# Folded constant's base part by POOL and VectorE, second half's mask ahead of the first fold, both first x2 roundings on ScalarE

## What is computed

```
x = x + L0: x @ ((sum_g y[b,g] * weight[g]) * mask).T + bias              # L0_cond_bias
x = x + L1: x @ W_base.T + b_base + 2 * (((x @ As.T) * y) @ Bs)           # LoRA of rank 16, 8 experts
x = x + L2: top-2 mixture of 8 gelu experts (width 512) + a shared expert
x = x + L3: one silu expert of width 256, chosen by argmax, with biases
```

```
c_b = (I + W_base) bias_l0  +  Bs.T ( cond_scaled[b] * (As bias_l0) )  +  b_base
```

## Time and profile before

| | |
|---|---|
| median of 3 runs | 139.98 us |
| runs | 138.63 to 140.18 us |
| the profiled execution: time | 138.68 us |
| the profiled execution: span | 136.9 us |
| TensorE matmuls busy | 132.6 us |
| VectorE busy | 102.2 us (75%) |
| ScalarE busy | 99.3 us (73%) |
| POOL busy | 75.3 us (55%) |

### The profile page before, as it was taken

The page is one execution under the profiler, slowest core; times in us unless marked ns, Lnnn a source line. Parts: engine busy times, 40 slices in busy tenths (PEclk is TensorE's granted clock), DMA queues, the critical chain, the costliest instruction groups (busy, mean ns, idle before and its releaser), DMA issues.

```text
span 136.9 us, 3163 instructions
## 1 busy us (share of the span) xinstructions
PE 132.6 (97%) x866; PEld 121.0 (88%) x866; DVE 102.2 (75%) x201; ACT 99.3 (73%) x205; POOL 75.3 (55%) x89
## 2 busy tenths in 40 slices
PE   6999999999999999999999999999999999999991
PEld 5978887878888899999999999999999999999990
DVE  0699898797766677578886787867868677887792
ACT  3774797969964669777797777756757669889870
POOL 0238369776991046477486774863542635325770
PEclk9999999999999999999999999999999999999999
DMA  4999999997001976564774656746577476565134
GB/s 139 343 403 408 409 400 397 403 400 304 4 0 74 385 304 266 229 255 187 306 290 180 268 217 279 287 186 268 208 286 296 171 306 242 210 249 226 41 115 153
DMA packets 11345, 34.54 MB, mean 252 GB/s; under 512 B 1088, under 2 KB 2368, under 8 KB 11328
## 3 DMA queue, kind: packets, MB, share of 16 engines
q1 hardware_dynamic: 11184, 34.21, 63.8%
q10 hardware_dynamic: 144, 0.13, 0.3%
HBM read 12.32 MB, written 1.05 MB: 98 GB/s over the span
## 4 chain that ended last, share of the span: by engine, by line
PE 97%; DVE 0%; issue 0%
PE up L293 34%; PE gate L293 32%; PE acc L293 31%; DVE x_res L997 0%; DVE slabs L827 0%; DVE shift_pick L828 0%
## 5 line engine op out<-in xcount | busy, mean ns | idle before, releaser
L766 POOL TENSOR_TENSOR dn_lo<-slabs,dn_hi 128x256 fp32r<-128x256 f32 x40 | 29.7, 742 | 41.0 <-ACT dn_hi L649 41.0
L625 ACT ACTIVATE h_act<-gate 128x512 f32<-128x512 f32 x48 | 28.8, 599 | 26.6 <-PE gate L293 25.2
L917 DVE TENSOR_TENSOR h_pair<-up,h_pair 128x512 fp32r<-128x512 f32 x55 | 37.5, 682 | 0.0
L927 DVE SCALAR_TENSOR_TENSOR up<-h_act,w_route,up 128x512 f32<-128x512 f32 x32 | 24.2, 755 | 16.9 <-PE up L293 16.9
L293 PE MATMUL gate<-x_hi,w_gu 128*128 128x256 f32 x160 | 35.3, 281 | 0.0
L293 PE MATMUL up<-x_hi,w_gu 128*128 128x256 f32 x158 | 34.9, 282 | 0.0
L631 ACT ACTIVATE h_pair<-up 128x512 fp32r<-128x512 f32 x55 | 32.8, 596 | 0.0
L293 PEld LDWEIGHTS gate<-x_hi,w_gu 128*128 128x128 f32 x160 | 27.5, 188 | 0.2
L293 PE MATMUL acc<-h_pair,dn_hi 128*128 128x512 f32 (+1 forms) x76 | 27.6, 378 | 0.0
L293 PEld LDWEIGHTS up<-x_hi,w_gu 128*128 128x128 f32 x158 | 27.1, 188 | 0.0
L293 PE MATMUL gate<-x_lo,w_gu 128*128 128x256 f32 x80 | 22.5, 282 | 0.0
(11 more groups left out here) (127 smaller groups left out, 204.1 us busy)
## 6 DMA issues: line engine op xcount, KB each, us to landing
w_gu<-slabs SPq DMA_DIRECT2D x40, 512.0 KB, 3.0
slabs<-slabs_moe SPq DMA_DIRECT2D x8, 768.0 KB, 13.1
slabs<-slabs_l SPq DMA_DIRECT2D x4, 768.0 KB, 8.4
outT<-x_res SPq DMA_DIRECT2D x7, 128.0 KB, 2.0
sh_raw<-slabs_shared SPq DMA_DIRECT2D x2, 384.0 KB, 5.2
x_res<-x_rest SPq DMA_DIRECT2D x1, 768.0 KB, 7.0
slabs<-second_in SPq DMA_DIRECT2D x1, 320.0 KB, 3.1
slabs<-third_in SPq DMA_DIRECT2D x1, 256.0 KB, 3.8
```

The source lines that it names most:

```text
L625: nc.scalar.activation(h_act[:, u % 2, :], gate_ps[u % 2][:], ACT.Gelu_apprx_tanh).then_inc(act_done, 1)
L766: nc.gpsimd.tensor_tensor(dn_lo[:, q % W_SLOTS, :], slab_cols(at, DOWN_AT, 256), dn_hi[:, q % W_SLOTS, :].bitcast(F32), ALU.subtract).then ...
L917: V.tensor_tensor(h_lo[:, u % H_SLOTS, :], h_of(u), h_hi[:, u % H_SLOTS, :].bitcast(F32), ALU.subtract).then_inc(h_lo_done, 1)
L927: ins = V.scalar_tensor_tensor(h_of(u), h_act[:, k, :], weight, h_of(u), ALU.mult, ALU.mult)
```

## The change

The constant's base part leaves TensorE. The host passes `L0_cond_bias` copied to all partitions as a row, and `W_base` untransposed. POOL multiplies two rows of 128, the A rows and W_base, by the bias row; VectorE sums each over its 128 inputs. The first sum is `As bias_l0` (one number per rank row), and `a_bias_y` is `cond_scaled` times it. The second is `W_base bias_l0`, and a new [128, 1] tensor `c_base` is it plus `bias_l0` plus `b_base`. TensorE keeps one of three 8-column products.

A transposed is no longer loaded. The A rows move from the third input to the fourth; the third shrinks to 192 KB, the fourth grows to 320 KB. The first `lora` on TensorE now waits for the fourth input.

`mask_w0(1, 2, 6)` moves ahead of the two first folds on VectorE. The second `x_hi` rounding moves from VectorE to ScalarE, behind the first and ahead of `round_shared(1)`.

```diff
         second_sb = early(5, P)
-        third_sb = early(4, P)
-        fourth_sb = early(3, P)
+        third_sb = early(3, P)
+        fourth_sb = early(5, P)
+        bias_terms = early(2, P)
...
-        lora_bT, mask, lora_a = second_sb[:, 4, :], third_sb[:, 2, :], third_sb[:, 3, :]
-        w_baseT, ident, lora_aT = (fourth_sb[:, k, :] for k in range(3))
+        lora_bT, mask = second_sb[:, 4, :], third_sb[:, 2, :]
+        w_baseT, ident, bias_row, lora_a = (fourth_sb[:, k, :] for k in range(4))
...
+            pe.wait_ge(d_fourth, DMA)
+
             def lora(out, first_b, n):
...
             lora(gate_ps[0][:, 0:S], 0, 2)
-            pe.wait_ge(d_fourth, DMA)
-            mm(acc_ps[:, 512:512 + B], lora_aT, bias_l0.to_broadcast([P, B]), True, True).then_inc(a_bias_sum, 1)
             pe.wait_ge(bw_ready, 2)
...
-            pe.wait_ge(base_ready, 1)
             pe.wait_ge(a_bias_ready, 1)
-            mm(acc_ps[:, 0:B], base_i[:], bias_l0.to_broadcast([P, B]), True, False)
-            mm(acc_ps[:, 0:B], lora_bT, a_bias_y[:], False, True).then_inc(c_sum, 1)
+            mm(acc_ps[:, 0:B], lora_bT, a_bias_y[:], True, True).then_inc(c_sum, 1)
...
             nc.scalar.activation(x_hi[:, 0:S], x2_ps(0), ACT.Identity, bias=c_b[:, 0:1]).then_inc(x2_hi_half, 1)
+            act.wait_ge(x2_first_sum, 2)
+            nc.scalar.activation(x_hi[:, S:2 * S], x2_ps(1), ACT.Identity, bias=c_b[:, 1:2]).then_inc(x2_hi, 1)
             round_shared(1)
...
             nc.gpsimd.tensor_tensor(base_i[:], ident, w_baseT, ALU.add).then_inc(base_ready, 1)
+            nc.gpsimd.tensor_tensor(bias_terms[:, :, :], fourth_sb[:, 3:5, :], rows(bias_row, 2),
+                                    ALU.mult).then_inc(bias_terms_ready, 1)
             pool.wait_ge(hit_ready, 1)
...
-            dve.wait_ge(a_bias_sum, 1)
-            V.tensor_tensor(a_bias_y[:], acc_ps[:, 512:512 + B], cond_scaled[:], ALU.mult).then_inc(a_bias_ready, 1)
             mask_w0(0, 2, 6)
+            dve.wait_ge(bias_terms_ready, 1)
+            V.tensor_reduce(bias_in[:], bias_terms[:, :, :], AX_X, ALU.add).then_inc(bias_in_ready, 1)
+            dve.wait_ge(bias_in_ready, 1)
+            V.tensor_scalar(a_bias_y[:], cond_scaled[:], bias_in[:, 0:1], None, ALU.mult).then_inc(a_bias_ready, 1)
+            mask_w0(1, 2, 6)
             dve.wait_ge(r1_first, 2)
             for b in range(2):
                 dve.wait_ge(m_first_sum, b + 1)
                 V.tensor_tensor(m_b[:, b, :], m_first_banks[b], r1_b[:, b, :], ALU.add).then_inc(m_first, 1)
-            mask_w0(1, 2, 6)
             add_base(1, 2, 4, gate_ps[1][:])
+            V.tensor_scalar(c_base[:], bias_in[:, 1:2], bias_l0, bias_l1, ALU.add, ALU.add).then_inc(c_base_ready, 1)
             dve.wait_ge(c_sum, 1)
-            V.tensor_scalar(c_b[:], acc_ps[:, 0:B], bias_l1, None, ALU.add).then_inc(acc_read, ACC_BIAS)
+            dve.wait_ge(c_base_ready, 1)
+            V.tensor_scalar(c_b[:], acc_ps[:, 0:B], c_base[:], None, ALU.add).then_inc(acc_read, ACC_BIAS)
             add_base(2, 6, 2, up_ps[1][:, 0:S])
...
-            dve.wait_ge(x2_first_sum, 2)
-            V.tensor_scalar(x_hi[:, S:2 * S], x2_ps(1), c_b[:, 1:2], None, ALU.add).then_inc(x2_hi, 1)
```

More of the change, by code:

```diff
@@ L117, in build @@
         a_bias_y = sb("a_bias_y", [P, B])
+        bias_in = sb("bias_in", [P, 2])
+        c_base = sb("c_base", [P, 1])
         w0_b = early(B, P)
@@ L190, in build @@
         r1_first, m_first_sum, m_first = sem("r1_first"), sem("m_first_sum"), sem("m_first")
-        a_bias_sum, a_bias_ready, c_sum = sem("a_bias_sum"), sem("a_bias_ready"), sem("c_sum")
+        bias_terms_ready, bias_in_ready, a_bias_ready, c_base_ready, c_sum = (
+            sem(n) for n in ("bias_terms_ready", "bias_in_ready", "a_bias_ready", "c_base_ready", "c_sum"))
         x2_first_sum, x2_sum, x2_ready, x2_hi_half, x2_hi, x2_lo = (
@@ L366, in x2 @@
                 pe.wait_ge(d_x_rest, DMA)
-                if p == 1:
-                    pe.wait_ge(a_bias_ready, 1)
-                else:
+                if p > 1:
                     pe.wait_ge(x2_ready, p)
@@ L1076 @@
     second = cat([w_l0[:, 2:6], a(L1_cond_Bs).transpose(0, 2, 1).reshape(P, 1, D)], axis=1)
-    third = cat([w_l0[:, 6:], a(L0_cond_mask)[:, None], as_[:, None]], axis=1)
-    fourth = np.stack([base, np.eye(P, dtype=np.float32), as_.T], axis=1)
+    third = cat([w_l0[:, 6:], a(L0_cond_mask)[:, None]], axis=1)
+    fourth = np.stack([base, np.eye(P, dtype=np.float32), np.broadcast_to(a(L0_cond_bias)[None], (P, D)),
+                       as_, a(L1_cond_W_base)], axis=1)
     chunks = [a(v).reshape(E, 2, P).transpose(2, 1, 0).reshape(P, 2 * E) for v in (L3_cond_b_up, L3_cond_b_gate)]
```

## The result

| | before | changed |
|---|---|---|
| median, 22 runs each | 139.07 us | 139.93 us |
| lowest to highest | 138.41 to 140.19 us | 139.52 to 142.19 us |
| ratio | | 1.0057, 95% interval [1.0037, 1.0078] |
| span of the profiled execution | 136.9 us | 137.8 us |
| first gate product starts (`gate<-x_hi,sh_hi`) | 11.33 us | 12.31 us |

The account below looks back on a forecast made before the run. VectorE was taken to pace the opening, up to the first gate product, with no slack behind it. Input +0.32 and VectorE's list +0.28 made +0.60 us on the runs' median of 139.98: 140.6 us, range 138.9 to 141.6.

Parts of the forecast that it names:

- VectorE paces the opening, and behind it there is no slack: Up to the first gate product at 11.33 us VectorE sets TensorE's pace; any later shift moves the end equally.
- Matmuls removed: Two 8-column L0-bias products leave TensorE in the opening, 0.14 us each; counted as nothing, being covered by VectorE's work.
- Later input: The first LoRA product waits for the larger fourth input, so VectorE's first base addition starts at 7.36, not 7.04: +0.32 us.
- VectorE's list: VectorE's instructions from the first base addition to that for the last two samples take 3.19 us instead of 2.91: +0.28.
- Both x_hi roundings on ScalarE, hidden: Two 0.47 us roundings on ScalarE end at 11.66 us, before TensorE asks at 11.93; no cost.
- TensorE's wait for x2: In the opening, TensorE's first x2 product can start after the first fold, at 9.62 us, 0.22 later than before.
- Port shared with POOL: Rival: POOL's sh_lo holds c_base on VectorE until 11.33 us, 0.96 us later; +1.56, 141.5 us; chance 0.1.
- Faster, TensorE late: Rival: TensorE's clock rises late in the opening, VectorE's idle time swallows the new instructions; 0.56 us less, 139.4 us; chance 0.25.
- The sum: Over the opening, 0.32 for the input plus 0.28 for VectorE's instructions: +0.60 us, 140.6 us.
- the case of no effect within 0.3 us: Case: input and VectorE costs in the opening at their low ends, within 0.3 us; 140.0 us; chance 0.15.

Follow-up runs that it names:

- without warm-up: The kernel before without its three warm-up matmuls on zeros: 140.29 us, 1.0105; the changed kernel without them: 141.95 us, 1.0213.
- the late warm execution: Profile of the kernel before with the first routed unit's weight address read ahead of the wait for the last expert's split: 138.89 us, 0.9995.
- 256 KB more: The kernel before with four unused copies of W_base added to the fourth input: 139.68 us, 1.0049.

## Why the prediction was right, and where it was off

**VectorE paces the opening, and behind it there is no slack: right.** 125.57 and 125.49 us remain behind the gate product, and TensorE's new idle times name VectorE. In six more profiles 125.50 to 125.57 us remain (12.10 to 137.6 with c_base early, for one); in the other six, from 125.7 to 126.65. The margin was thin, though: VectorE held TensorE up by only some 0.4 us before.

**Matmuls removed, counted at nothing: right.** The folds' products end at 8.29 + 0.39 = 8.68 and VectorE comes to them at 9.40.

**Later input: +0.32 forecast, +0.44 in the profiled pair, right only for executions like that one.** The landing was taken 0.20 us later and was 0.31 (6.69 against 6.38), more than my upper bound of 0.25. The LoRA product's start was forecast at 6.69 and came at 6.67, its two matmuls took 0.70 us instead of 0.60 since their weights could not be loaded ahead, and from their end to the addition it is 0.10 us in both kernels, where I had added 0.07: by my own rows the term should have read 0.35. What I missed is that the start is set by whichever is last, L0 products or input. Before, without that wait, the input came in time; in the profile with x_hi back on VectorE it came in time for the changed kernel too, and the term was nothing. The landings scatter: with before's inputs base_i started at 6.38, 6.29, 6.56, 5.80 and 6.14 us in five profiles (mean 6.23), with the changed one's at 6.69, 6.71, 6.22, 6.49 and 6.61 (mean 6.54; 6.14 with the same bytes and the A rows in the third), and once on each side at 8.47 and 8.01. The LoRA product's start shows no such shift: 6.67, 6.68, 6.34, 6.76 and 6.62 us in the five warm profiles of the changed order, mean 6.61, against 6.62 for the four of before's.

**VectorE's list: +0.28 forecast, +0.54 measured.** This is the term that was mis-sized; it lay even above my high end of 0.48. Reduction (0.44 to the dependent start, 0.45 forecast), masks (0.47 each), folds and the wide addition came as forecast. Of the 0.26 us that were missing, 0.21 are c_base: I had 0.19 us for it and its dependence, after the short a_bias_y of before, and it took 0.40: 0.26 us for the row, although it has a single element, and 0.14 until c_b starts. c_b waits for two semaphores there, which may be why the 0.04 of a single wait was not enough. With c_base early both waits have long been met, and c_b follows the wide addition after 0.60 us (9.99 to 10.59), as with one wait before (0.59): two waits cost nothing by themselves. What the second costs when it is the last to be met, no run separates from the rest. a_bias_y, 0.07 forecast, took 0.14.

**Both x_hi roundings on ScalarE, hidden: right**, by the run that undoes it. TensorE's wait for x2 was forecast at 9.62 and came at 9.82.

**Port shared with POOL (chance 0.1): did not happen.** One element was not held in any profile; two were, in the one execution that was tried.

**Faster, TensorE late (0.25): refuted as a mechanism.** I overlooked that VectorE's list and TensorE's folds hang on the same LoRA product, so that the idle time of 0.28 us stays 0.27 without warm-up and 0.28 in the late warm execution. Its chance should have been near 0.05.

**The sum** of +0.60 was right in sign and near in size: 0.86 us between medians of 22 (0.5 to 1.1 us by the interval, which leaves out the case of no effect within 0.3 us). 0.54 of it is the longer list, found in every profile of the changed inputs and order (3.45 or 3.46 us, against 2.90 or 2.91 in three with the order of before; 2.77 with 256 KB more, where the late input takes up a part of the idle time). A rest of about 0.3 us is not explained by a measurement. The interval alone would allow it to be nothing, but the three other kernels with this list and the warm-up, of 7 to 12 executions each, lie as high (1.0052 to 1.0071). The later input, with its wait of 0.30 us in executions with a late landing, is the candidate. But the kernel with the A rows back in the third input, whose LoRA product need not wait, lies as high (1.0064), and the profiles are too few to settle it: where the rest comes from stays open. In the profiled pair the forecast was 0.38 us short, 0.12 of it the input and 0.26 the list, and that the medians came nearer (0.26 short) owes something to luck.

## What to carry to other kernels

On an engine that paces by a list of small dependent instructions, taking work from an engine that waits anyway brings nothing unless the list gets shorter, and here it was a loss: count what each new instruction costs the next one, start to start, with its wait, and not its elements. Before filling an idle time, see what ends it; if both sides wait for one producer, the idle time is fixed and can be filled once, by one of the candidates. When something new must be waited for, ask which of the things already waited for comes last: the new wait costs nothing while another is later, and its full length when it is not. A value that is needed late is best computed early, several instructions ahead of its reader (0.22 us of list here).

## What the runs showed of the hardware

- A VectorE scalar instruction over SBUF with 2 elements per partition ended 0.02 us after a POOL instruction that ran beside it (0.85 us, one execution); with 1 element it took 0.26 or 0.27 us, beside POOL or not.
- On VectorE an instruction that waits for its forerunner's result starts 0.03 to 0.04 us after that has ended (8.35 + 0.41 = 8.76 to 8.79); c_b, with two waits, started 0.14 us after. An instruction that waits for nothing new started 0.07 us behind a small [128, 8] product (7.45 to 7.52) and 0.14 behind another (8.79 to 8.93).
- Reducing 256 inputs takes 0.41 us, on the line through 64 (0.21) and 320 (0.48).
- A [128, 8] multiply with a per-partition scalar from SBUF takes 0.23 us, the one with a constant 0.17 (`cond_scaled`, L830 of the kernel before).
- The landing of the same early loads moves between executions: base_i started between 5.80 and 6.56 us in five profiles, and two of thirteen profiles had it 1.5 to 2.2 us later than the others' mean.
- With the same warm-up, the twelve weight loads of the L0 products took 190 to 333 ns on average in different executions, while the granted clock read 1.00.
